# A recommendation tower on one core: dot products of two samples in one matmul, layers in the dot products' banks, another first stage

## What is computed

```python
combined = jnp.concatenate([dense_features[:, None, :], sparse_features], axis=1)
interactions = jnp.einsum('bnd,bmd->bnm', combined, combined)
z = jnp.concatenate([dense_features, interactions[:, _TRIU_I, _TRIU_J]], axis=1)
h = jnp.concatenate([z, r_dense_features], axis=1)
h = jnp.maximum(h @ W_top1 + b_top1, 0.0)     # 607 x 512
h = jnp.maximum(h @ W_top2 + b_top2, 0.0)     # 512 x 256
y = h @ W_top3                                # 256 x 1
```

## Time and profile before

| | |
|---|---|
| median of three runs | 597.74 us |
| profiled execution | 598.93 us |
| its span | 597.2 us |
| mean granted TensorE clock | 0.842 |
| instructions | 14574 |
| moved by DMA | 28.02 MB |

### The profile page before, as it was taken

The page is one execution under the profiler, slowest core; times in us unless marked ns, Lnnn a source line. Parts: engine busy times, 40 slices in busy tenths (PEclk is TensorE's granted clock), DMA queues, the critical chain, the costliest instruction groups (busy, mean ns, idle before and its releaser), DMA issues.

```text
span 597.2 us, 14574 instructions
## 1 busy us (share of the span) xinstructions
PE 466.2 (78%) x6057; PEld 423.9 (71%) x6057; DVE 256.7 (43%) x465; ACT 176.1 (29%) x443; POOL 296.0 (50%) x314
## 2 busy tenths in 40 slices
PE   3564677697988889676997979688797969977787
PEld 1463666586977878576886868677686858877776
DVE  3853458251544446252452626344262623622340
ACT  1231233332324332132322314132232423224341
POOL 7777144554554455455554545555554554545200
PEclk9557689897878988888888979869797796988899
DMA  5453211111111111111111111111111111111000
GB/s 116 157 171 88 73 27 39 38 44 37 36 45 35 42 37 46 38 38 42 36 46 33 46 33 44 38 35 42 41 45 37 33 45 32 41 37 38 23 3 1
DMA packets 19577, 28.02 MB, mean 47 GB/s; under 512 B 10691, under 2 KB 13267, under 8 KB 19518
## 3 DMA queue, kind: packets, MB, share of 16 engines
q0 software_dynamic: 9728, 19.94, 12.7%
q1 hardware_dynamic: 9790, 7.17, 4.1%
HBM read 27.08 MB, written 0.01 MB: 45 GB/s over the span
## 4 chain that ended last, share of the span: by engine, by line
PE 71%; issue 15%; ACT 3%; DMA 3%; another core or an unknown queue 3%; DVE 3%; SPq 1%; DVEq 0%; ACTq 0%
PE dots_ps L394 27%; PE fetch_ps L419 22%; PE h_ps L466 9%; PE vec_ps L372 6%; PE h_ps L482 4%; DMA vecs<-in_tbl 3%; PE ids_ps L401 2%; ACT vecs L607 1%; PE fetch_ps L466 1%; DVE onehot L739 1%; ACT inter L643 1%; DVE inter L818 1%; DVE vecs L590 1%; ACT vecs L590 0%
## 5 line engine op out<-in xcount | busy, mean ns | idle before, releaser
L333 POOL DMA_INDIRECT rows<-in_tbl,idx x304 | 293.5, 965 | 262.5 <-DMA rows<-in_tbl,idx 154.4
L394 PE MATMUL dots_ps<-vecs 128*27 128x27 f32 x4096 | 162.3, 202 | 73.1 <-issue 71.6
L394 PEld LDWEIGHTS dots_ps<-vecs 128*27 128x27 f32 x4096 | 148.1, 118 | 88.4 <-issue 85.8
L419 PE MATMUL fetch_ps<-onehot,t_hi 125*128 125x256 f32 x448 | 136.0, 327 | 38.4 <-ACT vecs L607 24.7
L818 DVE COPY_PREDICATED inter<-mask,dots_ps 27x128 f32<-27x128 int32 (+2 forms) x256 | 66.7, 260 | 205.4 <-ACT inter L643 198.9
L739 DVE TENSOR_TENSOR onehot<-ids_ps,row_of 125x1024 fp32r<-125x1024 f32 x94 | 111.2, 1220 | 59.5 <-PE ids_ps L401 32.6
L419 PE MATMUL fetch_ps<-onehot,t_lo 125*128 125x256 f32 x448 | 133.5, 326 | 0.0
L419 PEld LDWEIGHTS fetch_ps<-onehot,t_hi 125*128 125x128 f32 x448 | 99.6, 222 | 43.0 <-issue 36.6
L643 ACT COPY inter<-dots_ps 27x128 f32<-27x128 f32 (+1 forms) x256 | 63.8, 249 | 179.9 <-PE dots_ps L394 106.1
L419 PEld LDWEIGHTS fetch_ps<-onehot,t_lo 125*128 125x128 f32 x448 | 100.0, 223 | 4.5 <-issue 0.2
L607 ACT COPY vecs<-fetch_ps 128x256 f32<-128x256 f32 x56 | 37.6, 672 | 125.8 <-PE fetch_ps L419 99.4
(11 more groups left out here) (65 smaller groups left out, 194.5 us busy)
## 6 DMA issues: line engine op xcount, KB each, us to landing
rows<-in_tbl,idx POOLq DMA_INDIRECT x304
vecs<-in_tbl SPq DMA_DIRECT2D x6, 500.0 KB
rows<-in_r_dense_features SPq DMA_DIRECT2D x16, 64.0 KB
h_sb<-in_W_top_laid SPq DMA_DIRECT2D x2, 512.0 KB
w_sb<-in_W_top SPq DMA_DIRECT2D x1, 512.0 KB
w_sb<-in_tbl SPq DMA_DIRECT2D x1, 500.0 KB
idx<-in_ids SPq DMA_DIRECT2D x16, 13.0 KB
w_dense<-in_W_top SPq DMA_DIRECT2D x1, 256.0 KB
```

The costliest lines, as they stand in the source:

```text
L333: nc.gpsimd.indirect_dma_start(out=rows[v % 2][:, s, :], out_offset=None, in_=tables[f - 1][:, :], in_offset=bass.IndirectOffsetOnAxis(ap= ...
L394: last = pe.matmul(dots_ps[q * 32:q * 32 + N, n // HALF, o:o + N], vs[:, b, :], vs[:, b, :], start=True, stop=True)
L419: last = pe.matmul(fetch_ps[:, 0:R], part[0:KP, k, h * KH + t, :], onehot[buf][h][0:KP, t, :], start=(h == 0 and t == 0 and part is t_hi), ...
```

## The change

- **Pairs.** `vecs` has 32 places a sample instead of 27, the last five zero. One matmul takes the 64 places of two samples as weights and their 2x27 vectors as moving operand, 64 a tile. Of its 64x54 result the two diagonal blocks are used. `dots_done` counts two halves of 64 samples, not four quarters, and GpSimd's groups 1 and 2 wait for the first and for both.
- **Banks.** `dots_ps` has four banks (8 pairs in each); `h1_ps` and `h2_ps` are gone. Layers 1 to 3 write the same four banks, so they wait until the products of the tile before are copied and merged (`dots_banks_free`), and `dots` waits for the rectified layer 1 or the kept y.
- **Order.** Fetches 0 and 1 stand among the first tile's transposes, layer 1 among the second's, layer 2 behind fetch 5, layer 3 behind fetch 6. VectorE compares items 5 and 6 behind the second tile's merge and x_lo. The next item's ids are spread in the second half of a fetch, always into the one bank `ids_ps`.
- **First stage.** The seven tables' ids come as rows laid out before the launch; each table is loaded in two pieces (112 and 13 partitions); fetches 4 and 5 stand among the transposes.
- **y as a row.** Layer 3 has the weights `w3` as stationary operand (one column) and 256 samples moving: 4 records; no transpose at the end.
- The space for descriptors of GpSimd's DMAs is 2048 bytes a partition; it was 16384.

```diff
+    NP = 32
+    PAIR = 2 * N
+    BANKS = 4
+    SLOTS = QS // BANKS
...
-        vecs = [sb(f"vecs{s}", [P, 2, P, N]) for s in range(2)]
+        vecs = [sb(f"vecs{s}", [P, 2, P, NP]) for s in range(2)]
...
-        dots_ps = ps("dots_ps", [P, 2, 512])
-
-        h1_ps = ps("h1_ps", [P, M1 // 2, R])
-        h2_ps = ps("h2_ps", [P, M2, R])
+        dots_ps = ps("dots_ps", [P, BANKS, 512])
...
-                        pool.wait_ge(dots_done, i * (4 * Q) + (v - 2) * Q + (0, 1, 4)[k])
+                        pool.wait_ge(dots_done, i * 8 + (v - 2) * 2 + k)
...
+            def dots_banks_free(i, v):
+
+                pe.wait_ge(inter_by_act, i * (4 * NA) + (v + 1) * NA)
+                pe.wait_ge(inter_by_dve, i * (4 * ND) + (v + 1) * ND)
+
             def dots(i, v):
...
-                for b in range(P):
-                    q, n = b // QS, b % QS
-                    o = (n % HALF) * N
-                    last = pe.matmul(dots_ps[q * 32:q * 32 + N, n // HALF, o:o + N], vs[:, b, :],
-                                     vs[:, b, :], start=True, stop=True)
-                    if n == QS - 1:
-                        last.then_inc(dots_done, 1)
...
+                if not (first and v < 2):
+
+                    if v % 2:
+                        pe.wait_ge(relu1_done, i * (2 * M1) + v // 2 * M1)
+                    elif not (first and v == 2):
+                        pe.wait_ge(y_kept, i * 2 + v // 2 - 1)
+                for h in range(2):
+                    for n in range(QS):
+                        o = n % SLOTS * PAIR
+                        b = h * 64 + n * 2
+                        last = pe.matmul(dots_ps[h * 64:h * 64 + 64, n // SLOTS, o:o + PAIR],
+                                         vs[:, b:b + 2, :].rearrange("p b f -> p (b f)"), vs[:, b:b + 2, 0:N],
+                                         start=True, stop=True)
+                    last.then_inc(dots_done, 1)
...
+                            if h == 1 and t == 0 and part is t_hi:
+
+                                if k < X - 1:
+                                    spread_ids(round_, k + 1)
+                                else:
+                                    spread_ids(round_ + 1, 0)
...
+                if not prev:
+                    fetch_first(range(4))
+                    pe.wait_ge(ident_made, 1)
+                transpose_rows(i, v, in_first_tile)
+                if not prev:
+                    fetch_first([6])
+                dots(i, v)
+                fetch_items(i, r, [2] if prev else [0])
+                transpose_rows(i, v + 1, in_second_tile)
+                fetch_items(i, r, [3])
+                dots(i, v + 1)
+                fetch_items(i, r, [4, 5])
                 if prev:
...
+                    layer2(*prev, False, lambda: dots_banks_free(i, v + 1))
+                fetch_items(i, r, [6])
+                if prev:
+                    layer3(*prev, False)
...
+                transpose_rows(i, 3, in_second_tile)
+                layer2(i, 0, True)
                 dots(i, 3)
...
+                layer3(i, 0, True)
+                layer1(i, 1, range(M1), lambda: dots_banks_free(i, 3))
+                layer2(i, 1, True)
...
                     split_input(i, v)
-                    keep_y(*prev)
-                    compare_items(i, r, LAST)
+                    compare_items(i, r, [4])
+                    merge_products(i, v + 1)
+                    split_input(i, v + 1)
+                    compare_items(i, r, [5, 6])
+                    keep_y(*prev, False)
...
-    nc = bacc.Bacc("TRN2", target_bir_lowering=False, num_devices=1)
+    nc = bacc.Bacc("TRN2", target_bir_lowering=False, num_devices=1, dynamic_dma_scratch_size=2048)
...
+    given["ids_spread"] = np.ascontiguousarray(given["ids"][:, [f - 1 for f in SPREAD]].T)
```

More of the change, by code:

```diff
@@ L435, in layer1 @@
-            def layer1(i, r, half, some=range(L1)):
-                spare = isinstance(i, int) and i == PASSES - 1
+                    fetch(k, *item(i, r, k), i * 2 + r + 1)
+            def layer1(i, r, ms, free):
                 tiles = i * 4 + (r + 1) * 2
-                bank = h1_half(half, spare)
-                for n in some:
-                    m, at = divmod(n, 3 * (JG + 1))
-                    c0 = (half * (M1 // 2) + m) * P
-                    if n == 0 and half == first_half(i, r):
+                for m in ms:
+                    if m == 0:
@@ L487, in layer3 @@
[L487 to L497 removed]
+                        free()
@@ new lines, in layer1 @@
+                    for at in range(3 * (JG + 1)):
+                        if at < 2 * (JG + 1):
+                            jj, w, x = at // 2, (w_hi, w_lo)[at % 2], x_hi
+                        else:
+                            jj, w, x = at - 2 * (JG + 1), w_hi, x_lo
+                        last = pe.matmul(h1_at(m), w[:, jj, m * P:(m + 1) * P], x[:, jj, :],
+                                         start=(at == 0), stop=(at == 3 * (JG + 1) - 1))
+                    last.then_inc(h1_done, 1)
@@ new lines, in layer2 @@
+            def layer2(i, r, spare, free=lambda: None):
+                pe.wait_ge(mlp_w_in, 64)
+                pe.wait_ge(relu1_done, i * (2 * M1) + (r + 1) * M1)
+                free()
+                for m in range(M2):
+                    for k in range(M1):
+                        last = pe.matmul(h2_at(m, spare), w2_sb[:, k, m * P:(m + 1) * P], h1_sb[:, k, :],
+                                         start=(k == 0), stop=(k == M1 - 1))
+                    last.then_inc(h2_done, 1)
@@ L675, in step @@
                 if prev:
[L676 to L684 removed]
+                    take_vectors(i, v, (0, 1))
```

539 lines of the change are left out of this document (218 added, 321 removed).

## The result

The changed kernel is slower: 615.33 us (median of four runs, 609.26 to 617.89) against 596.88 us for the old one beside it, a ratio of 1.029 with a 95% interval of 1.019 to 1.040. The forecast was 581, with a range of 566 to 607. The profiled execution is the fastest of the four: 609.26 us, span 607.5.

A forecast was written before the change was run, and what follows sets the result against it. The prediction took TensorE's dot products, starved of supply while GpSimd makes gather descriptors, as the bound. Its terms -7.3-10.8-5.0+5.3+1.2 = -16.6 us gave 581 us from 597.7, range 566 to 607.

The forecast's parts named there:

- Part 3: First stage, to dots 2: chained fetches start earlier, the gap before dots 2 grows; -7.3 us, bounds -16 and +7.
- Part 2: Work beside the dots: new waits against shorter stretches; 67.5 us a round, -10.8 for six, -5 in the last.
- What bounds the kernel: Opening step: TensorE's dot products are starved while GpSimd makes descriptors; the gathers' floor lies close behind.
- The trickle: TensorE's dots: while GpSimd makes descriptors, supply falls to a trickle and TensorE lives on 40 to 57 queued records.
- the second bound: GpSimd's paced gathers: 33.9 us a tile, 67.8 a round, said not to bind within six rounds.
- Part 1: Dots, two samples in one matmul: 54 ns a record, loop stretches from 15.5 to 11 us, bounds 9 and 13.8.
- the same block: First stage: dots 0 would begin at 51 and stick until 62, where unpaced gathers hold the engines today.
- rival B: Loop rounds: fetch 5's wait and the half clock it costs make a round 71.3 us, total 607; chance 0.14.
- Rival D: First stage gains nothing because the block moves with the fetches: 588 us; chance 0.11.
- Part 4: The end: +5.3 us from dots 14 to dots 15, +1.2 after dots 15.
- Rival A: GpSimd's gathers become the bound, ending at 535, with the kernel at 573 us; chance 0.18.
- Rival C: Dots: trickle goes by time, or load and matmul stand in line; stretch 13.8, total 623 us; chance 0.12.

The follow-up runs named there:

- best2: Changed kernel with last-step layers moved, unstrided inter, earlier compare 5, later x_lo wait, fewer GpSimd waits for tiles 2, 3 and 15: 614.65 us, ratio 1.039.
- after_ctrl: The changed kernel unaltered, run again in the third set, without standstills: 589.85 us in one run, ratio 1.018 to the old kernel's 579.60.

## Why the prediction was wrong

Three steps failed, in this order of size: Part 3's -7.3 us measured +9.5; in Part 2 the wait for the banks, 0.3 us a round, measured 3.2; and the floor of the gathers was taken not to bind.

**What bounds the kernel** was half right. The trickle was read correctly, and best2 shows it bare. But the second bound was set aside too soon: "GpSimd is one to two tiles ahead of TensorE, so this floor does not bind within six rounds". The chain was priced at 33.9 us a tile and takes 35.0 to 35.3, 70 us a round or more, above the 67.5 that the prediction gave TensorE; and the lead has to last to the end, not six rounds. The best case shows it: after_ctrl has dots 0 at 50.3 and stretches of 7.5 us, both better than forecast, and still takes 589.85 us, because the last gather ends at 544.1 and 44.0 us lie behind it. Without gathers the old kernel takes 434 us: TensorE's own need is 150 us below the time, and the rest is gathers, through the chain or through standstills. With the chain where it was, a faster TensorE had 7 to 9 us to gain, not 16.6, and the changed kernel's chain began later.

**Part 1** held: stretches of 9.1 us on average, the loop's 9.4 to 9.8, against the 11 taken. A term that came out better than forecast did not save the sum. One reading in it was loose: the 48 records of 42 ns stood "at half clock", but the granted clock over them (312.0 to 314.1) was 0.77.

**Part 2** is the step that failed in the rounds: "banks before layer 1, 0.3" measured 4.6 us a round in the first profile, 2.5 in each of the other two with standstills, and 1.2 without gathers. The 0.3 was the wait for copies that start on time and merges as fast as the old ones. Of the 4.80 us shown above, ScalarE's start behind gathers in a row took 3.7, and VectorE's strided merge 0.8 (3.17 us for eight where the old kernel takes 2.34 for as many). The old trace held the first: those 68.9 us for "remote". I saw no harm in it and did not ask who would wait for them once banks are shared. The three profiles with different bank waits have equal rounds (68.0, 68.1, 68.1): what the standstills do not take there they take in fetches and dots. With the last round's -5 taken out (it held: -5.9), a full round is 69.1 us against 67.5: 19.3 in the stretches where 22 was taken, and 49.8 outside where 45.5 was, of which the bank wait is 2.9. Fetch 5's wait was right (4.2 against 4.89), and rival B's mechanism is real: the clock falls behind it, and without gathers that costs 2.8 us a round, not 1.1.

**Part 3** failed most, by 16.8 us, the size of the whole forecast gain. The fetches' chain was right (dots 0 at 50.3 without standstills), but "would stick in the same block until 62" was wrong: the block is no place but lasts as long as the unpaced gathers, and two fetches of a serial chain are caught in it (9.35 and 14.11 us). Rival D, which said that the block moves with the fetches, was nearer, but kept the later gains. "-3.3 and -3.2" for dots 0 and 1 held (-6.6 for both), but the gap between them, -1.5, measured +4.1, and the gap before dots 2, +5.7, measured +8.1: +5.6 for all; without gathers the step is 12.4 longer. (That last gap was misread too: dots 1 of the old kernel end at 113.7, not 112.84, so it was 18.4 and not 19.3.) The weight splits, compares and merges stand in line on VectorE there, behind one bank of ids. The descriptor space at nothing was 0.5% where I could measure it.

**Part 4**: +5.3 for dots 14 to dots 15 measured +5.5. After dots 15 I had +1.2 and got +4.3: layer 1 waits 5.4 us for x_lo, behind two quadrants and the slower merge.

**Rival A** named the right floor with the wrong price: it ended the gathers at 535 and the kernel at 573, 38 us later. Measured are 544.1 and 44.0 at best, and 561 to 569 and 47 with standstills. Rival C (a record that takes twice as long) is out.

## What to carry to other kernels

An engine whose idle time is only waiting for its own transfers is at its limit, and work saved on another engine is lost beside it beyond the lead that it has; add up that engine's pace to its last transfer, put what must follow behind it, and compare with the forecast. When buffers are merged, price the wait by when the last reader really starts in the trace, stalls included, not by how long it runs. Put the unchanged kernel beside every variant in the same set: two of six sets lacked a stall that the other four had, and a single comparison would have given a layout the credit.

## What the runs showed of the hardware

- Beside GpSimd's indirect gathers in a row TensorE, ScalarE and VectorE are held up in some sets of runs and not in others, with the same kernel: stretches of 7.5 us against 9.1, dots 0 at 50.3 against 74.0. With 21 in a row TensorE got 18 records in 17.6 us.
- The old kernel's median was 580 and 587 us in the sets without standstills and 597 to 605 with them; the changed kernel's 590 and 615 to 618.
- COPY_PREDICATED from a bank to every second fp32 takes 437 ns for 128 numbers and 296 to neighbouring ones.
- A record with 64 weight columns and 54 moving ones takes 58 ns at full clock (7.48 us for 128), no less than the two with 27 and 27 that it replaces (27.1 ns each).
